# Two of the four transfers that exchange a tile's exponentials move from SyncE's queue to ScalarE's

## The chip, the cores and the metric

The kernel runs on one core of a Trainium2 chip. The metric is the device time of one execution in microseconds, lower is better. Engines are named as in the profile: PE is TensorE, DVE is VectorE, ACT is ScalarE, POOL is GpSimd, SP is SyncE. An engine's name with a q behind it (ACTq, SPq) is its sequencer, which waits, branches and issues DMAs.

## What is computed

x is 8 x 1024 x 1024, ctx 8 x 64 x 1024, everything in f32:

```
x = x + xattn(layernorm(x), ctx, mask)
x = x + ffn(layernorm(x), weight, lora_A, lora_B, router_w)

xattn(h, mem, mask):   scores  = einsum('bsd,bmd->bsm', h, mem) / sqrt(1024)
                       scores  = where(mask[:, None, :], scores, -1e30)
                       readout = einsum('bsm,bmd->bsd', softmax(scores), mem)
                       (zero for a batch entry without a valid key)
ffn(x, weight, ...):   base    = einsum('btd,od->bto', x, weight)
                       probs   = softmax(einsum('btd,ed->bte', x, router_w))
                       the two largest of 8 experts, renormed, into w_dense
                       Ax      = einsum('nd,erd->ner', x_flat, lora_A)     # rank 16
                       out     = base + 2.0 * einsum('ner,ne,eor->no', Ax, w_dense, lora_B)
```

## The kernel before

The 8192 rows of x are 64 tiles of 128 rows, 8 tiles (j = 0 to 7) in each of 8 batch entries. PE multiplies in fp32r: each f32 operand is split in a high part and a low rest, and a product is three matmuls (high x high, high x low, low x high; three, L1097). All weights stay in SBUF. A tile passes through stages that overlap with those of its neighbours; each engine has a step function that is called for every tile in turn (unrolled for the first and last batch entry, in a loop over the others), and within an engine the instructions run strictly in the order written there. Nothing but semaphores ties the engines together.

In step (tile) the engines do work of five tiles. With nxt, nxt2, +3 for the tiles 1, 2 and 3 later:

- PE (step, L1224): the three groups of base columns of the tile, 24 products (L1100 to L1102; group 0 holds the router logits and the LoRA columns too); after an odd j the scores of two later tiles (pair_scores, L1127 and L1129); the readout of nxt2 (L1174 and L1175, weights are eT); lora_second of the tile (weights are hT_hi and hT_lo).
- DVE (step, L986): softmax_split and e_transposes of nxt2, an xT_low, router_top (L929), router_gate (L941 to L960), h_transposes, x2_transposes of nxt (L914), add_readout and norm2_stats of nxt2, hT_low (L968), norm2_moments, x2T_low of nxt (L921), softmax_scores of +3, and the base additions (L984).
- ACT (step, L660): the two exponentials of nxt2 (L581, L583), norm1_mean (L552) and norm1_squares (L559) of +3, gate_exp of the tile (L617), eT_copy of nxt2 (L588), x2T_high of nxt (L613), hT_high of the tile (L623), in an odd j two xT_high, and norm2 of nxt2, which writes xn (L607).
- POOL: the powers and products of both norms, a few elements each.
- SP (step, L424): all transfers. exchange (L375) copies xn to xq in four DMAs; then e_exchange (L411), store (L370), h_exchange (L405), the load of a later tile's x, in an even j s_exchange, in an odd one two loads of xT.

Once per batch entry the context changes: in j = 3 DVE sums the new ctxT and SP has loaded it just before; in j = 4 PE makes the mean (L1107), DVE subtracts it (ctx_centre, L780) between h_transposes and x2_transposes, and ACT makes the high part (ctxT_high, L533) between gate_exp and eT_copy; in j = 5 DVE makes the new mask.

The exchange of the exponentials. A transpose on DVE turns blocks of 32 x 32 only. e_transposes (L869) writes the tile's 128 x 128 values of e_split, turned block by block, into eq, and counts eq_done up. e_exchange then puts the four bands of 32 partitions side by side with four DMAs of 16 KB each:

```
def e_exchange(tile):
    sp.wait_ge(eq_done, count(tile, 1, 1 - 5))
    for i in range(Q):
        sp.dma_start(e_raw[:, i * QP:(i + 1) * QP], eq[i * QP:(i + 1) * QP, :]).then_inc(e_loaded, 16)
```

eT_copy on ACT waits until e_loaded has counted all four (16 * Q per tile) and rounds e_raw into eT, the weights of the readout. The first five tiles are turned on PE instead and have no such exchange. eq and e_raw are parts of the tensor w_raw, so in the profile the transfers read w_raw<-w_raw (L415), and eT_copy reads eT<-w_raw. s_exchange is w_raw<-w_raw too (L421).

norm1_mean and norm1_squares each pass over a tile's 128 x 1024 values; what they write beside their sums goes into x2T, which x2_transposes overwrites later: that one waits until the squares are counted in ln1_step.

Of the kernel before, what the change touches and what calls it, by code (L numbers as in the profile page):

```python
# [23 lines left out]
def xattn_lora_moe_kernel(  # L24
# [17 lines left out]

    P = 128
    NT, _, D = x_in.shape
    NB, _, _, M = ctxT_in.shape
    ER, O = bT_in.shape
    WC = wT_in.shape[2]
# [12 lines left out]
    Q = 4  # L60
    QP = P // Q
# [24 lines left out]
    def count(tile, per, more=0):  # L86

        b, j = tile
        return b * (TPB * per) + (j * per + more)

    def after(tile, n):
        return (tile[0], tile[1] + n)

    def exists(tile):
        return not isinstance(tile[0], int) or tile[0] * TPB + tile[1] < NT

    def turned_on_pe(tile, n):
        return isinstance(tile[0], int) and tile[0] * TPB + tile[1] < n

    def slot(tile):  # L100
        return tile[1] % XS
# [7 lines left out]
    with stack:  # L109
# [6 lines left out]
        def sem(name):  # L116
            return stack.enter_context(nc.semaphore(name))
# [73 lines left out]
        eq = w_raw[0][:, C - 1, P:2 * P]  # L191
        e_raw = w_raw[0][:, C - 1, 2 * P:3 * P]
# [13 lines left out]
        def x(tile):  # L206

            i = slot(tile) - XF
            if i < 0:
                return x_first[:, slot(tile), :]  # L210
            return x_rest[i][:, :, :].rearrange("p c n -> p (c n)")[:, x_from[i]:x_from[i] + D]
# [108 lines left out]
        eq_done = sem("eq_done")  # L320
        e_loaded = sem("e_loaded")
# [28 lines left out]
        def _(sp):  # L350
# [60 lines left out]
            def e_exchange(tile):  # L411

                sp.wait_ge(eq_done, count(tile, 1, 1 - 5))
                for i in range(Q):
                    sp.dma_start(e_raw[:, i * QP:(i + 1) * QP], eq[i * QP:(i + 1) * QP, :]).then_inc(e_loaded, 16)  # L415

            def s_exchange(tile):
# [6 lines left out]
            def step(tile, first=False):  # L424
# [4 lines left out]
                if exists(after(tile, 3)) and not first and not turned_on_pe(after(tile, 3), 5):  # L429
                    e_exchange(after(tile, 3))  # L430
# [99 lines left out]
        def _(act):  # L530
            def ctxT_high(b):
                act.wait_ge(ctx_centred, b + 1)
                act.copy(ctxT[:, :, 0:M], ctxT_raw[:, :, :]).then_inc(ctxT_hi_done, 1)  # L533

            def ctx_high(b):
                act.wait_ge(ctx_loaded, b * 16 + 16)
                if isinstance(b, int) and b == 0:
                    act.wait_ge(ctx_rest_loaded, 16)
                act.wait_ge(readout_done, count((b, 0), 2))
                act.copy(ctx_hi[:, :], ctx_raw[:, 0:D]).then_inc(ctx_hi_done, 1)  # L540

            def norm1_mean(tile):
                b, j = tile
                xs = x(tile)
                junk = x2T[:, :, :].rearrange("p c n -> p (c n)")
                act.wait_ge(x_loaded[slot(tile)], b * (16 * TPB // XS) + 16 * (j // XS + 1))
                if isinstance(b, int) and tile == (0, 0):
                    act.wait_ge(x_rest_loaded[0], 16)
                act.wait_ge(rstd1_done, count(tile, 1))
                if not isinstance(b, int) or b > 0 or j > 1:  # L550
                    act.wait_ge(x2T_split, count(tile, 2, -4))
                act.activation(junk, xs, ACT.Identity, scale=-1.0 / D, accum_out=neg_mean1[:, :]).then_inc(ln1_step, 1)  # L552

            def norm1_squares(tile):

                xs = x(tile)
                junk = x2T[:, :, :].rearrange("p c n -> p (c n)")
                act.wait_ge(ln1_step, count(tile, 2, 1))
                act.activation(junk, xs, ACT.Square, bias=neg_mean1[:, :], accum_out=sum_sq1[:, :]).then_inc(ln1_step, 1)  # L559

            def xT_high(tile, i):
                b, j = tile
                k = j // 2 % 2
                act.wait_ge(xT_loaded[k][i], b * (16 * TPB // 4) + 16 * (j // 4 + 1))
                if isinstance(b, int) and tile == (0, 0):
                    act.wait_ge(xT_rest_loaded[i], 16)
                act.wait_ge(sT_done, pairs(tile, 1))
                act.copy(xT_hi[:, i], xT_raw[:, k, i]).then_inc(xT_hi_done, 1)  # L568
# [6 lines left out]
            def softmax_exp(tile):  # L575
                act.wait_ge(softmax_step, count(tile, 5, 3))
                if turned_on_pe(tile, 6):
                    act.wait_ge(eT_done, count(tile, 1))
                else:
                    act.wait_ge(eq_done, count(tile, 1, -5))  # L580
                act.activation(e_all[:, :], s_all[:, :], ACT.Exp, bias=neg_max[:, :],  # L581
                               accum_out=e_sum[:, :]).then_inc(exp_done, 1)
                act.activation(e_split[:, 0:M], s_all[:, :], ACT.Exp, bias=neg_max[:, :]).then_inc(exp_done, 1)  # L583

            def eT_copy(tile):
                act.wait_ge(e_loaded, count(tile, 16 * Q, 16 * Q * (1 - 5)))
                act.wait_ge(readout_done, count(tile, 2))
                act.copy(eT[:, :], e_raw).then_inc(eT_copied, 1)  # L588

            def first_softmax_exp(tile):  # L590
                act.wait_ge(softmax_step, count(tile, 5, 3))
                act.wait_ge(e_split_done, count(tile, 1))
                act.wait_ge(x1_done, count(tile, 2))
                act.wait_ge(eT_done, count(tile, 1))
                act.activation(e_all[:, :], s_all[:, :], ACT.Exp, bias=neg_max[:, :],
                               accum_out=e_sum[:, :]).then_inc(exp_done, 1)
                act.activation(first_e(0), by_blocks(s_all[:, :]), ACT.Exp, bias=neg_max[:, :]).then_inc(exp_done, 1)

            def first_eT_copy(tile):
                act.wait_ge(eT_done, count(tile, 1, 1))  # L600
                act.wait_ge(readout_done, count(tile, 2))
                act.copy(eT[:, :], et_ps).then_inc(eT_copied, 1)

            def norm2(tile):
                act.wait_ge(shift2_done, count(tile, 1, 1))
                act.wait_ge(x2T_done, count(tile, TS))
                act.activation(xn[:, :], x(tile), ACT.Identity, bias=shift2[:, :],  # L607
                               scale=rstd2[:, :]).then_inc(xn_done, 1)

            def x2T_high(tile):  # L610
                act.wait_ge(x2T_done, count(tile, TS, TS))
                for i in range(2):
                    act.copy(chunks(xT2_hi[:, tile[1] % 2], i), chunks(x2T, i)).then_inc(x2T_hi_done, 1)  # L613

            def gate_exp(tile):
                act.wait_ge(router_step, count(tile, 7, 1))
                act.activation(gate_num[:, :], top8[:, 0:1], ACT.Exp, bias=top8[:, 1:2],  # L617
                               scale=-1.0).then_inc(gate_exp_done, 1)

            def hT_high(tile):  # L620
                act.wait_ge(h_loaded, count(tile, 16 * Q, 16 * Q * (1 - 2)))
                act.wait_ge(base_done, count(tile, G))
                act.copy(hT_hi[:, :], h[:, :]).then_inc(hT_hi_done, 1)  # L623
# [36 lines left out]
            def step(tile):  # L660
                b, j = tile
                nxt, nxt2 = after(tile, 1), after(tile, 2)
                if turned_on_pe(nxt2, 5):
                    first_softmax_exp(nxt2)
                elif exists(nxt2):
                    softmax_exp(nxt2)
                if exists(after(tile, 3)):
                    norm1_mean(after(tile, 3))
                    norm1_squares(after(tile, 3))
                gate_exp(tile)  # L670
                if j == TPB - 4 and exists((b, TPB)):
                    ctxT_high(b + 1)
                if turned_on_pe(nxt2, 5):
                    first_eT_copy(nxt2)
                elif exists(nxt2):
                    eT_copy(nxt2)
                if exists(nxt):
                    x2T_high(nxt)
                hT_high(tile)
                if j == TPB - 3 and exists((b, TPB)):  # L680
                    ctx_high(b + 1)
                if j % 2 == 1 and exists(after(tile, 5)):
                    for i in range(2):
                        xT_high(after(tile, 5), i)
                if exists(nxt2):
                    norm2(nxt2)
# [701 lines left out]
```

## Time and profile before

| | |
|---|---|
| median of 3 runs | 984.8 us (983.56 to 985.69) |
| profiled execution | 983.3 us, span 981.2 us |
| PE busy | 973.7 us (99%) |
| PE weight loads busy | 961.7 us (98%) |
| DVE busy | 850.0 us (87%) |
| ACT busy | 474.5 us (48%) |
| POOL busy | 144.2 us (15%) |
| DMA | 160 GB/s in the mean |

The span runs from the first instruction to the last one's end. A matmul's duration in the rows below (about 0.33 us) is longer than its distance to the next one (about 0.16 us), since they are pipelined; distances are read from starts. Rows of a timeline give the start in us from the span's start, the duration, engine, line, operation, out<-in, shape and count, and in brackets how long the engine was idle before it and what ended that.

### The profile page before, as it was taken

What the parts mean: (1) busy time and instruction counts of PE and PEld (TensorE: products, weight loads), DVE (VectorE), ACT (ScalarE), POOL (GpSimd) and SP (SyncE); (2) the same over time, 40 slices, a digit from 0 to 9 for tenths busy, and PEclk for the clock granted to TensorE, in tenths of its full rate; (3) what the DMA queues carried; (4) which work ended last, traced back from release to release, by engine and by line L of the source; (5) the groups of instructions that cost most, each with busy time, mean ns of one, the idle gap of its engine ahead of it and who ended that gap; (6) DMA issues with size and microseconds to landing.
All of it is one profiled execution on the core that took longest, in us unless ns stands there. A gap on an engine that the chain in (4) does not pass through costs nothing.

```text
span 981.2 us, 18824 instructions
## 1 busy us (share of the span) xinstructions
PE 973.7 (99%) x6081; PEld 961.7 (98%) x6081; DVE 850.0 (87%) x2201; ACT 474.5 (48%) x930; POOL 144.2 (15%) x278
## 2 busy tenths in 40 slices
PE   8999999999999999999999999999999999999998
PEld 7999999999999999999999999999999999999998
DVE  6988988889888998889988899888998889888774
ACT  6755544545444455445455445454454454453420
POOL 3311111111111111111111111111111111111110
PEclk9999999999999999999999999999999999999999
DMA  9646565655566555565555755556655566554522
GB/s 323 216 131 166 157 172 159 179 132 153 165 175 181 164 124 160 165 193 157 154 137 156 203 138 169 140 140 196 162 161 163 124 191 168 160 159 127 122 67 76
DMA packets 156095, 156.61 MB, mean 160 GB/s; under 512 B 93968, under 2 KB 128912, under 8 KB 156048
## 3 DMA queue, kind: packets, MB, share of 16 engines
q1 hardware_dynamic: 155184, 154.63, 56.8%
q10 hardware_dynamic: 864, 1.45, 0.4%
q8 instruction: 18, 0.29, 0.1%
q14 instruction: 29, 0.24, 0.1%
HBM read 78.74 MB, written 33.55 MB: 114 GB/s over the span
## 4 chain that ended last, share of the span: by engine, by line
PE 89%; DVE 5%; DMA 2%; issue 1%; SPq 1%; ACT 1%; POOL 0%; ACTq 0%; DVEq 0%; POOLq 0%
PE base_ps L1100 26%; PE base_ps L1101 25%; PE base_ps L1102 25%; PE ro_ps L1174 3%; PE ro_ps L1175 3%; PE s_ps L1129 2%; PE s_ps L1127 2%; PE base_ps L1206 1%; DMA xq<-xn 1%; DVE stats L898 1%; DMA xT_raw<-in_xT 1%; DVE x2T L914 1%; DVE w_raw L892 1%; SPq L379 1%; ACT xn L607 0%
## 5 line engine op out<-in xcount | busy, mean ns | idle before, releaser
L1100 PE MATMUL base_ps<-w_hi,xT_hi 128*128 128x392 f32 x1512 | 495.5, 328 | 0.0
L1101 PE MATMUL base_ps<-w_lo,xT_hi 128*128 128x392 f32 x1512 | 494.4, 327 | 0.0
L1102 PE MATMUL base_ps<-w_hi,xT_lo 128*128 128x392 f32 x1512 | 494.4, 327 | 0.0
L1100 PEld LDWEIGHTS base_ps<-w_hi,xT_hi 128*128 128x128 f32 x1512 | 285.8, 189 | 1.7
L1101 PEld LDWEIGHTS base_ps<-w_lo,xT_hi 128*128 128x128 f32 x1512 | 285.8, 189 | 1.6
L1102 PEld LDWEIGHTS base_ps<-w_hi,xT_lo 128*128 128x128 f32 x1512 | 285.8, 189 | 0.0
L914 DVE STREAM_TRANSPOSE x2T<-xq 128x512 f32<-128x512 f32 x122 | 166.1, 1465 | 19.7 <-DMA xq<-xn 19.4
L492 POOL TENSOR_TENSOR rstd<-var_eps,neg_half 128x1 f32<-128x1 f32 x64 | 61.8, 966 | 504.1 <-DVE var_eps L905 504.1
L613 ACT CAST xT_hi<-x2T 128x512 fp32r<-128x512 f32 x122 | 69.5, 617 | 106.2 <-DVE x2T L914 106.2
L588 ACT CAST eT<-w_raw 128x128 fp32r<-128x128 f32 x59 | 17.6, 299 | 151.7 <-DMA w_raw<-w_raw 151.7
L921 DVE TENSOR_TENSOR xT_lo<-x2T,xT_hi 128x512 fp32r<-128x512 f32 x122 | 78.3, 682 | 0.0
L607 ACT ACTIVATE xn<-w_raw,shift,rstd 128x1024 f32<-128x1024 f32 x32 | 39.7, 1241 | 70.9 <-POOL shift L495 70.9
L814 DVE TENSOR_TENSOR xT_parts<-xT_raw,xT_parts 128x1024 fp32r<-128x1024 f32 x62 | 73.4, 1186 | 0.0
L607 ACT ACTIVATE xn<-x_first,shift,rstd 128x1024 f32<-128x1024 f32 x29 | 36.0, 1241 | 69.4 <-POOL shift L495 69.4
L568 ACT CAST xT_parts<-xT_raw 128x1024 fp32r<-128x1024 f32 x64 | 63.8, 1042 | 0.0
L1100 PE MATMUL base_ps<-b_hi,hT_hi 128*128 128x384 f32 (+1 forms) x192 | 59.7, 311 | 0.9 <-DVE hT_lo L968 0.9
L1102 PE MATMUL base_ps<-b_hi,hT_lo 128*128 128x384 f32 (+1 forms) x192 | 59.3, 309 | 0.0
L1101 PE MATMUL base_ps<-b_lo,hT_hi 128*128 128x384 f32 (+1 forms) x192 | 59.3, 309 | 0.0
L486 POOL TENSOR_TENSOR var_eps<-sum_sq,eps_sum 128x1 f32<-128x1 f32 x64 | 17.4, 272 | 277.8 <-ACT x2T L559 276.8
L1129 PE MATMUL s_ps<-xT_parts,ctxT 128*128 128x256 f32 x232 | 53.3, 275 | 0.0
L1127 PE MATMUL s_ps<-xT_parts,ctxT 128*128 128x256 f32 x232 | 53.2, 275 | 0.0
L929 DVE MAX8 top<-base_ps 128x8 f32<-128x8 f32 x64 | 11.1, 173 | 45.0 <-PE base_ps L1102 44.3
(132 smaller groups left out, 1391.5 us busy)
## 6 DMA issues: line engine op xcount, KB each, us to landing
xT_raw<-in_xT SPq DMA_DIRECT2D x62, 512.0 KB, 5.3
xq<-xn SPq DMA_DIRECT2D x244, 128.0 KB, 3.5
w_raw<-in_x SPq DMA_DIRECT2D x32, 512.0 KB, 3.5
out<-x_first SPq DMA_DIRECT2D x32, 512.0 KB, 2.7
out<-w_raw SPq DMA_DIRECT2D x31, 512.0 KB, 2.8
x_first<-in_x SPq DMA_DIRECT2D x30, 512.0 KB, 3.6
h<-w_raw SPq DMA_DIRECT2D x248, 16.0 KB, 2.0
w_raw<-w_raw SPq DMA_DIRECT2D x236, 16.0 KB, 2.6
```

What stands on the lines that cost most here:

```text
L492: pool.tensor_tensor(rstd2[:, :], var_eps2[:, :], neg_half[:, :], ALU.pow).then_inc(rstd2_done, 1)
L568: act.copy(xT_hi[:, i], xT_raw[:, k, i]).then_inc(xT_hi_done, 1)
L607: act.activation(xn[:, :], x(tile), ACT.Identity, bias=shift2[:, :], scale=rstd2[:, :]).then_inc(xn_done, 1)
L613: act.copy(chunks(xT2_hi[:, tile[1] % 2], i), chunks(x2T, i)).then_inc(x2T_hi_done, 1)
L814: dve.tensor_tensor(xT_lo[:, i], xT_raw[:, tile[1] // 2 % 2, i], xT_hi[:, i].bitcast(f32), ALU.subtract).then_inc(xT_split, 1)
L914: dve.transpose(out_[:, i * QS:(i + 1) * QS], xq[:, i * QS:(i + 1) * QS, :].rearrange("p g (c n) -> p g c n", n=QP)).then_inc(x2T_done, 1)
L921: dve.tensor_tensor(chunks(xT2_lo[:, k], i), chunks(x2T, i), chunks(xT2_hi[:, k], i).bitcast(f32), ALU.subtract).then_inc(x2T_split, 1)
L1100: pe.matmul(out_, a_hi, w_h, start=start, stop=False, skip_group_check=again)
L1101: pe.matmul(out_, a_hi, w_l, start=False, stop=False, skip_group_check=again)
L1102: return pe.matmul(out_, a_lo, w_h, start=False, stop=stop, skip_group_check=again)
L1127: pe.matmul(s_ps[:, 0:T2], ctxT[:, c, :], xT_hi[:, :, c, :].rearrange("p t n -> p n t"), start=(c == 0), stop=False)
L1129: mm = pe.matmul(s_ps[:, 0:T2], ctxT[:, c, :], xT_lo[:, :, c, :].rearrange("p t n -> p n t"), start=False, stop=(c == C - 1))
```

## The change

SP issues the first two of the four transfers of e_exchange; the last two are issued by ACT, between norm1_mean and norm1_squares of its step, after a wait of its own for eq_done. The count that eT_copy waits for is the same.

```diff
@@ block.sync, e_exchange @@
                 sp.wait_ge(eq_done, count(tile, 1, 1 - 5))
-                for i in range(Q):
+                for i in range(Q // 2):
                     sp.dma_start(e_raw[:, i * QP:(i + 1) * QP], eq[i * QP:(i + 1) * QP, :]).then_inc(e_loaded, 16)
@@ block.scalar @@
+            def e_exchange(tile):
+                act.wait_ge(eq_done, count(tile, 1, 1 - 5))
+                for i in range(Q // 2, Q):
+                    act.dma_start(e_raw[:, i * QP:(i + 1) * QP], eq[i * QP:(i + 1) * QP, :]).then_inc(e_loaded, 16)
+
@@ block.scalar, step @@
                 if exists(after(tile, 3)):
                     norm1_mean(after(tile, 3))
+                if exists(nxt2) and not turned_on_pe(nxt2, 5):
+                    e_exchange(nxt2)
+                if exists(after(tile, 3)):
                     norm1_squares(after(tile, 3))
                 gate_exp(tile)
```

ACT's instructions in the step j = 4 of the first batch entry, before. The names are those of the lists above; top is the sorted logits, ctxT the context's high part:

```order
L581 ACTIVATE e_all,e_sum<-s_all,neg_max 128x64 [waits eq_done,softmax_step]
L583 ACTIVATE e_split<-s_all,neg_max 128x64
L552 ACTIVATE x2T,neg_mean<-w_raw 128x1024 [waits x2T_split,rstd1_done,x_loaded7]
L559 ACTIVATE x2T,sum_sq<-w_raw,neg_mean 128x1024 [waits ln1_step]
L617 ACTIVATE gate_num<-top 128x1 [waits router_step]
L533 CAST ctxT<-ctxT_raw 128x8x64 [waits ctx_centred]
L588 CAST eT<-w_raw 128x128 [waits readout_done,e_loaded]
```

The same place with the change:

```order
L581 ACTIVATE e_all,e_sum<-s_all,neg_max 128x64 [waits eq_done,softmax_step]
L583 ACTIVATE e_split<-s_all,neg_max 128x64
L552 ACTIVATE x2T,neg_mean<-w_raw 128x1024 [waits x2T_split,rstd1_done,x_loaded7]
L588 DMA w_raw<-w_raw 128x1x32 [waits eq_done]
L588 DMA w_raw<-w_raw 128x1x32
L559 ACTIVATE x2T,sum_sq<-w_raw,neg_mean 128x1024 [waits ln1_step]
L622 ACTIVATE gate_num<-top 128x1 [waits router_step]
L533 CAST ctxT<-ctxT_raw 128x8x64 [waits ctx_centred]
L593 CAST eT<-w_raw 128x128 [waits readout_done,e_loaded]
```

Two issues with a wait for eq_done stand between the passes; the rest keeps its order (lines below the insertion have numbers that are 5 higher).

SP's queue in one step with an odd j, before (xq<-xn is exchange, L415 e_exchange, out the store, h the h_exchange):

```order
L379 DMA xq<-xn 32x4x256 [waits xn_done]
L379 DMA xq<-xn 32x4x256 x3
L415 DMA w_raw<-w_raw 128x1x32 [waits eq_done]
L415 DMA w_raw<-w_raw 128x1x32 x3
L373 DMA out<-x_first 128x1024 [waits out_done]
L409 DMA h<-w_raw 128x1x32 [waits hq_done]
```

And with the change:

```order
L379 DMA xq<-xn 32x4x256 [waits xn_done]
L379 DMA xq<-xn 32x4x256 x3
L415 DMA w_raw<-w_raw 128x1x32 [waits eq_done]
L415 DMA w_raw<-w_raw 128x1x32
L373 DMA out<-x_first 128x1024 [waits out_done]
L409 DMA h<-w_raw 128x1x32 [waits hq_done]
```

The store and h_exchange follow after two issues of e_exchange instead of four.

## Rows read from the trace of the kernel before

**Rows 1.** Windows: stretch, length; busy us (count) of PE, PEld, DVE, ACT, POOL; PEclk, DMA, GB/s.

```profile
360.00:480.00 120.00, 120.00 (x754) 119.14 (x754) 107.05 (x277) 59.00 (x116) 16.85 (x32) 1.00 0.59 161
```

**Rows 2.** Waits of the whole span: engine, line, awaited: us in total, times, longest.

```profile
ACT eT L588 <- DMA w_raw<-w_raw: 151.7, 52, 4.4
...
DVE hT_lo L968 <- ACT hT_hi L623: 5.7, 3, 4.1
...
PEld ro_ps L1174 <- ACT eT L588: 1.6, 5, 0.4
```

**Rows 3.** Timeline of PE: the first matmul of the readout in two long steps.

```profile
410.82 0.38 PE L1174 MATMUL ro_ps<-ctx_hi,eT 128*128 128x512 f32 x1
...
440.52 0.38 PE L1174 MATMUL ro_ps<-ctx_hi,eT 128*128 128x512 f32 x1
```

**Rows 4.** Timeline of ACT through an ordinary long and short step.

```profile
400.96 1.24 ACT L607 ACTIVATE xn<-x_first,shift,rstd 128x1024 f32<-128x1024 f32 x1 [3.02 <-POOL shift L495]
...
405.66 0.30 ACT L617 ACTIVATE gate_num<-top 128x1 f32<-128x1 f32 x1 [0.57 <-DVE top L929]
...
416.34 1.24 ACT L607 ACTIVATE xn<-x_first,shift,rstd 128x1024 f32<-128x1024 f32 x1 [2.08 <-POOL shift L495]
...
419.00 0.19 ACT L552 ACTIVATION_READ_ACCUMULATOR x2T<-w_raw 128x1 f32 x1
...
421.40 0.29 ACT L617 ACTIVATE gate_num<-top 128x1 f32<-128x1 f32 x1 [0.93 <-DVE top L929]
...
430.65 1.24 ACT L607 ACTIVATE xn<-w_raw,shift,rstd 128x1024 f32<-128x1024 f32 x1 [3.03 <-POOL shift L495]
```

**Rows 5.** Timeline of DVE through the same two steps.

```profile
407.67 2.61 DVE L914 STREAM_TRANSPOSE x2T<-xq 128x512 f32<-128x512 f32 x2
411.02 0.45 DVE L873 STREAM_TRANSPOSE w_raw<-s_ps 128x256 f32<-128x256 f32 x1 [0.74 <-PE s_ps L1129]
...
418.59 0.31 DVE L869 STREAM_TRANSPOSE w_raw<-e_split 128x128 f32<-128x128 f32 x1
...
423.32 2.76 DVE L914 STREAM_TRANSPOSE x2T<-xq 128x512 f32<-128x512 f32 x2
...
428.48 0.27 DVE L968 TENSOR_TENSOR hT_lo<-h,hT_hi 128x128 fp32r<-128x128 f32 x1
```

**Rows 6.** Timeline of PE's weight loads: the first of lora_second in that short step.

```profile
429.38 0.19 PEld L1100 LDWEIGHTS base_ps<-b_hi,hT_hi 128*128 128x128 f32 x1
```

**Rows 7.** One line's instructions (ns min/median/max), and the page's issues (median us to landing).

```profile
L415 SPq DMA_DIRECT2D w_raw<-w_raw x236: 542/605/1117, 77.5 to 943.3; - x118
...
w_raw<-w_raw SPq DMA_DIRECT2D x236, 16.0 KB, 2.6
```

**Rows 8.** Timeline of ACT and of PE's weight loads in a step j = 4.

```profile
451.09 0.29 ACT L617 ACTIVATE gate_num<-top 128x1 f32<-128x1 f32 x1 [0.48 <-DVE top L929]
...
454.21 0.29 ACT L588 CAST eT<-w_raw 128x128 fp32r<-128x128 f32 x1
...
454.56 0.19 PEld L1174 LDWEIGHTS ro_ps<-ctx_hi,eT 128*128 128x128 f32 x1
```

**Rows 9.** Timeline of ACT at the start: the first of its six issues, and its first work.

```profile
0.74 0.41 ACTq L688 DMA_DIRECT2D ctxT_raw<-in_ctxT  x1
...
3.69 1.28 ACT L695 ACT_TABLE_LOAD   x1 [3.69 <-issue]
```

**Rows 10.** Timeline of ACT and PE's weight loads in another step j = 4.

```profile
213.13 0.30 ACT L617 ACTIVATE gate_num<-top 128x1 f32<-128x1 f32 x1
...
216.60 0.19 PEld L1174 LDWEIGHTS ro_ps<-ctx_hi,eT 128*128 128x128 f32 x1 [0.42 <-ACT eT L588]
```

**Rows 11.** Timeline of ACT and DVE in the steps j = 5 and j = 6.

```profile
465.33 0.28 ACT L617 ACTIVATE gate_num<-top 128x1 f32<-128x1 f32 x1
...
468.15 2.64 DVE L914 STREAM_TRANSPOSE x2T<-xq 128x512 f32<-128x512 f32 x2 [0.46 <-DMA xq<-xn]
...
481.01 0.30 ACT L617 ACTIVATE gate_num<-top 128x1 f32<-128x1 f32 x1 [1.04 <-DVE top L929]
```

## The prediction

> **What bounds the kernel now.** The page in the table above says that PE is busy 973.7 of 981.2 us, DVE 850.0, ACT 474.5. The windows say whether that leaves slack anywhere in the middle: in a stretch of 120 us PE is busy 120.00, at a granted clock of 1.00 [rows 1]. The waits come next: in the middle of the kernel PE waits only for five weight loads of the readout that eT holds up, 1.6 us in all [rows 2]. So PE sets the time. What helps another engine can give back little more than those 1.6 us; what makes PE wait is paid in full.
>
> The question is how closely the others follow PE. An even j takes a short step, an odd one a long step (with pair_scores). From one long step's readout to the next PE takes 440.52 - 410.82 = 29.70 us [rows 3]. Beside it runs a ring of ACT, DVE and POOL that closes once per step: xn (L607), exponentials, the two passes of norm 1, gate_exp (L617), router_gate, x2_transposes (L914), readout and stats, POOL, and the next xn. I walk it by the starts in the timeline and take out the idle time in which an engine waited for something that PE decides:
> - long step: from xn at 400.96 to gate_exp at 405.66, less 0.57 idle, 4.13; to x2T at 407.67, 2.01; to the next xn at 416.34, 8.67, less 0.74 in which DVE waited for PE's scores, 7.93. Sum 14.07 [rows 4, 5].
> - short step: from 416.34 to 421.40 less 0.93, 4.13; to x2T at 423.32, 1.92; to xn at 430.65, 7.33. Sum 13.38 [rows 4, 5].
>
> The ring needs 27.45 us in each 29.70 of PE: 2.25 us are free in two steps. PE meets the ring's work at three places, the weight loads of the readout (after eT), of lora_second (after hT_lo) and of the next base. hT_lo ends at 428.48 + 0.27 = 428.75 and the load behind it starts at 429.38 [rows 5, 6]: 0.63 us of margin.
>
> **The change, part by part.** SP loses two of four small issues per tile, 605 ns each by the median [rows 7], so 1.21 us. xq is issued ahead of e_exchange and stays where it was. Behind it the store and h_exchange move up; neither is worth anything, for hT_lo waited for ACT's side of that path 5.7 us in three places only [rows 2]. What is won is eT: ACT waits for its data 151.7 us in 52 places [rows 2], and the last transfer is now issued some 1.2 us earlier. That shortens ACT's idle time. PE has of it only what lies in late readouts outside the step j = 4; one of 0.42 lies inside [rows 10], and I take 0.6 of the 1.6 for the rest. Gain: 0.6 us.
>
> ACT gains one wait and two issues in every step, between mean and squares. On ACT the squares, gate_exp and all later work are queued behind them; router_gate and x2_transposes on DVE wait for gate_exp. The wait costs nothing in an ordinary step: the transposed exponentials end at 418.59 + 0.31 = 418.90, before the mean's accumulator read starts at 419.00 [rows 4, 5]. For the issues no row shows a small SBUF-to-SBUF transfer on ACT's queue. The nearest are the same transfer on SP, 542 to 1117 ns, median 605 [rows 7], and ACT's six larger loads at the start, the first 0.41, all six from 0.74 to 3.69, when ACT's first work starts [rows 9]: an issue holds ACT. I take the same transfer's 2 x 0.605 = 1.21, less 0.06 beside the accumulator read: **1.15 us per step**. The bounds are 0.82 (2 x 0.41) and 2.23 (2 x 1.117), and below these nothing, should ACT compute on while it issues.
>
> That time is not spare. The ring becomes 27.45 + 2 x 1.15 = 29.75 against PE's 29.70. An ordinary pair of steps breaks even: late, inside the 0.63 margin, with nothing left to catch up. So whatever stretches the ring once per batch reaches PE, and seven batches have these steps:
> - j = 4. ctx_centre and ctxT_high (L533) stand between the gate and eT. gate_exp had 0.48 of idle, so it comes 1.15 - 0.48 = 0.67 later, and all behind it moves along: L533, then eT, which ended at 454.21 + 0.29 = 454.50, with PE's weight load at 454.56 [rows 8]. There is no margin; PE waits 0.67. In three of the seven (the one near 213 stands in [rows 10]; also near 570 and 690) gate_exp had no idle and eT was late already: there all of 1.15 is paid. 4 x 0.67 + 3 x 1.15 = 6.1 us.
> - j = 5 and 6. In j = 5 gate_exp had no idle, so it is 1.15 later, of which x2T's 0.46 of waiting for xq absorbs a part: 0.69. In j = 6 gate_exp had 1.04: 0.11 more [rows 11]. That makes 0.80 against 0.63 at lora_second: 0.17 x 7 = 1.2 us.
>
> Sum: 6.1 + 1.2 - 0.6 = **+6.7 us**. The profiled execution took 983.3 us, so 990.0 for it; the median of the three runs shown is 984.8, which gives **991.5**.
>
> The Trainium skill, "DMA: Bandwidth & Descriptors", section "Issuing engines are not separate DMA queues", says that starting DMAs on several engines saves only the sequencer's time to start them, which is usually small beside the DMA. By it alone, nothing would be won or paid. This trace does not agree on "small": 0.605 us of issue beside 2.6 to landing [rows 7], and it is paid on an engine that has the ring behind it.
>
> **The rivals.**
> - Cheap issue: 0.41 each, 0.82 per step, as ACT's loads at the start. Against it: the median of SP's issues of just this kind is half as long again. The ring is 29.09 and recovers between batches; the steps j = 4 remain: 4 x (0.82 - 0.48) + 3 x 0.82 = 3.8, less 0.6: +3.2, 988.0. Chance 0.22.
> - Dear issue: ACT issues while SP issues xq, and the two slow each other to 1.117 each. The ring is 27.45 + 4.46 = 31.91, 2.21 over PE in each of 29 pairs (236 / 4 = 59 tiles): +64, 1049. Against it: at the start both queues issue side by side at 0.41 to 0.54, and 1.117 is one of 236 [rows 7, 9]. Chance 0.08.
> - Not slower: ACT's engine works on while the issues run, or they slip under the mean's pass. Then only the earlier eT is left, 0.6 to 1.6 off: 983.2 to 984.2. It decides if less than 0.48 per step is added, the idle time in j = 4. For it: the exponentials are ready before the mean is done. Against it: ACT takes its queue in order, and [rows 9]. Chance 0.17, 0.04 of it for a gain over 2 us, which PE's waits hardly hold. The rule of the Trainium skill above would come out here too.
> - The ring as forecast: 0.53. Within it, 1.27 per step instead of 1.15 makes 29.99, 0.29 over PE in 29 pairs: 8 us more, 1000.
>
> **How the numbers follow.** The likeliest case gives 991.5. The range 984.0 to 1003.0 leaves out the dear issue (0.08) and about half of the case without cost (0.09). A measurement of this kernel can tell some 0.2%, 2 us, from no change. Slower by more: ring, cheap and dear issue, less 0.03 that fall short of it, 0.80. Within: 0.16. Faster by more: 0.04.
>
> **What would show it.** In the profile after: two issues on ACT's queue per step between L552 and L559, about 0.6 each, and L559's start 1.2 us later behind L552; ACT's idle time before gate_exp nearly gone; DVE idle behind gate_exp; ACT's wait for eT's data down by half or more; and PE's weight loads waiting for eT in all seven steps j = 4, 0.7 to 1.2 each, and at times for hT_lo. I am wrong if the issues on ACT take under 0.4, if L559 does not move, or if the time grows while PE's waits stay at 1.6 us.

## The result, and the profile after

The changed kernel takes 991.15 us (median of 6 runs, 989.92 to 993.95) against 984.69 of the kernel before on the same chip; the ratio is 1.0070, 95% interval 1.0059 to 1.0081. That is 6.5 us more. 991.5 was forecast.

The page of the kernel after, its busy times:

```profile
span 989.6 us, 18848 instructions
...
PE 973.1 (98%) x6081; PEld 959.2 (97%) x6081; DVE 850.2 (86%) x2201; ACT 464.8 (47%) x930; POOL 141.6 (14%) x278
```

No engine has more work than before (DVE's 850.2 against 850.0 is the largest difference upwards). The span is 8.4 us longer than the 981.2 before, and PE is busy as long as it was; so the time came as idle time of PE. The window that answers to [rows 1]:

```profile
360.00:480.00 120.00, 118.86 (x745) 117.70 (x744) 105.40 (x276) 56.37 (x114) 16.13 (x32) 1.00 0.60 160
```

PE lost 1.14 us in these 120 us, at the same granted clock. The stretch is as long as one batch entry and holds one step j = 4. The waits (engine, line, awaited: us in total, times, longest) say for whom it waits; line numbers are 5 (ACT) or 8 (DVE, PE) higher than before:

```profile
ACT eT L593 <- DMA w_raw<-w_raw: 129.9, 52, 3.8
...
ACT x2T L559 <- issue: 66.4, 58, 1.6
...
DVE gate_den L949 <- ACT gate_num L622: 23.6, 37, 1.1
DVE x2T L922 <- DMA xq<-xn: 19.5, 40, 1.4
...
ACT gate_num L622 <- DVE top L937: 12.4, 4, 6.3
PEld ro_ps L1182 <- ACT eT L593: 10.5, 10, 1.7
...
PEld base_ps L1108 <- DVE hT_lo L976: 1.8, 3, 1.3
```

PE's weight loads wait 10.5 us for eT where they waited 1.6 [rows 2]: 8.9 us more, while the span grew by 8.4. Two rows lead up to it. ACT stands idle ahead of the squares (L559) for 66.4 us in 58 steps, behind the issues, and gate_den on DVE, which never waited for gate_num before, does so for 23.6 us. One row refutes a step of the forecast: ACT still waits 129.9 us for the data of eT, against 151.7, where half or less was forecast.

The timeline of ACT in an ordinary short step, the counterpart of [rows 4]:

```profile
419.65 1.24 ACT L612 ACTIVATE xn<-x_first,shift,rstd 128x1024 f32<-128x1024 f32 x1 [1.90 <-POOL shift L495]
...
421.37 1.04 ACT L552 ACTIVATE x2T<-w_raw 128x1024 f32<-128x1024 f32 x1
422.24 0.57 ACTq L588 DMA_DIRECT2D w_raw<-w_raw  x1
...
422.85 0.62 ACTq L588 DMA_DIRECT2D w_raw<-w_raw  x1
423.58 1.15 ACT L559 ACTIVATE x2T<-w_raw,neg_mean 128x1024 f32<-128x1024 f32 x1 [1.08 <-issue]
...
424.74 0.28 ACT L622 ACTIVATE gate_num<-top 128x1 f32<-128x1 f32 x1
...
427.35 0.30 ACT L593 CAST eT<-w_raw 128x128 fp32r<-128x128 f32 x1 [2.33 <-DMA w_raw<-w_raw]
```

The first issue starts at 422.24, beside the end of the mean (421.37 + 1.04 = 422.41). The squares start 2.21 us after the mean. Before they did so after 1.16:

```profile
418.06 1.04 ACT L552 ACTIVATE x2T<-w_raw 128x1024 f32<-128x1024 f32 x1
...
419.22 1.15 ACT L559 ACTIVATE x2T<-w_raw,neg_mean 128x1024 f32<-128x1024 f32 x1
...
424.06 0.30 ACT L588 CAST eT<-w_raw 128x128 fp32r<-128x128 f32 x1 [2.37 <-DMA w_raw<-w_raw]
```

So ACT is held 1.05 us. That is about the idle time of 0.93 that gate_exp had in this step: no bracket stands behind L622 any more, and it starts 3.37 us after the mean (424.74 - 421.37), where it started 3.34 after it before (421.40 - 418.06). The last row says what became of the gain. From xn to eT_copy it took 424.06 - 416.34 = 7.72 us before and takes 427.35 - 419.65 = 7.70 now. The data of eT is there not a bit earlier. The instructions of one line, ACT's issues:

```profile
L588 ACTq DMA_DIRECT2D w_raw<-w_raw x118: 550/616/894, 75.7 to 948.8; - x118
...
DMA to landing us min/median/max: 3.1/3.5/4.1
```

An issue costs ACT 616 ns, where it cost SP 605 [rows 7]. But eT_copy waits for the last of the four transfers, and that is none of ACT's: in all 59 exchanges SP's second lands last now, as SP's fourth did before. This last transfer in the step shown, after and then before:

```profile
L415 SPq DMA_DIRECT2D w_raw<-w_raw x1: 617/617/617, 424.3 to 424.3; - x1
...
DMA to landing us min/median/max: 3.0/3.0/3.0
```

```profile
L415 SPq DMA_DIRECT2D w_raw<-w_raw x1: 602/602/602, 422.1 to 422.1; - x1
...
DMA to landing us min/median/max: 1.8/1.8/1.8
```

It was issued 5.8 us after xn's start and is issued 4.6 us after it now (422.1 - 416.34 and 424.3 - 419.65), 1.2 earlier as forecast; but it takes 3.0 us to land where it took 1.8. Both sums are 7.6. The last xq transfer lands later too, 5.95 us after xq's first issue in the median, against 5.58. Which part of the DMA side holds the eight transfers to the same end isn't shown.

The step j = 4 that answers to [rows 8], from the timeline of ACT, DVE and PE's weight loads:

```profile
452.17 1.04 ACT L552 ACTIVATE x2T<-w_raw 128x1024 f32<-128x1024 f32 x1
...
453.12 0.30 DVE L877 STREAM_TRANSPOSE w_raw<-e_split 128x128 f32<-128x128 f32 x1
...
453.46 1.27 ACTq L588 DMA_DIRECT2D w_raw<-w_raw  x2
...
454.84 1.15 ACT L559 ACTIVATE x2T<-w_raw,neg_mean 128x1024 f32<-128x1024 f32 x1 [1.54 <-issue]
...
455.99 0.28 ACT L622 ACTIVATE gate_num<-top 128x1 f32<-128x1 f32 x1
...
456.30 0.15 DVE L949 TENSOR_SCALAR gate_den<-gate_num 128x1 f32<-128x1 f32 x1 [1.09 <-ACT gate_num L622]
...
458.44 0.62 ACT L533 CAST ctxT<-ctxT_raw 128x512 fp32r<-128x512 f32 x1 [2.18 <-DVE ctxT_raw L788]
458.97 0.29 ACT L593 CAST eT<-w_raw 128x128 fp32r<-128x128 f32 x1
459.31 0.19 PEld L1182 LDWEIGHTS ro_ps<-ctx_hi,eT 128*128 128x128 f32 x1 [1.44 <-ACT eT L593]
```

Here the transposed exponentials end at 453.42, 0.2 us behind the mean (453.21), and the issue waits for them: the squares start 2.67 us after the mean, 1.50 later than before (449.37 - 448.20 = 1.17). gate_exp is late by more than its idle time, DVE waits 1.09 at gate_den, and the chain L788, L533, eT hands the lateness on to PE, which waits 1.44.

### The profile page after: what moved, and what is told of

The parts are those of the page before. It is cut to its first block, busy times and chain, and to the rows that moved or that the text cites. A ratio compares the mean times of both kernels' runs of the same rounds, so it can differ in the third digit from the quotient of the medians.

```text
span 989.6 us, 18848 instructions
## 1 busy us (share of the span) xinstructions
PE 973.1 (98%) x6081; PEld 959.2 (97%) x6081; DVE 850.2 (86%) x2201; ACT 464.8 (47%) x930; POOL 141.6 (14%) x278
## 4 chain that ended last, share of the span: by engine, by line
PE 30%; DVE 23%; issue 16%; DMA 13%; POOL 5%; ACT 5%; SPq 5%; ACTq 2%; POOLq 0%; DVEq 0%
DMA xq<-xn 12%; PE base_ps L1108 8%; PE base_ps L1110 8%; PE base_ps L1109 8%; DVE stats L906 5%; SPq L379 5%; DVE x2T L922 5%; POOL rstd L492 4%; ACT xn L612 3%; DVE w_raw L900 3%; DVE x_first L900 2%; ACTq L588 1%; PE base_ps L1214 1%; POOL shift L495 1%; PE ro_ps L1182 1%
## 5 line engine op out<-in xcount | busy, mean ns | idle before, releaser
L922 DVE STREAM_TRANSPOSE x2T<-xq 128x512 f32<-128x512 f32 x122 | 164.6, 1453 | 20.0 <-DMA xq<-xn 19.5
L593 ACT CAST eT<-w_raw 128x128 fp32r<-128x128 f32 x59 | 17.6, 298 | 129.9 <-DMA w_raw<-w_raw 129.9
L486 POOL TENSOR_TENSOR var_eps<-sum_sq,eps_sum 128x1 f32<-128x1 f32 x64 | 13.5, 211 | 341.1 <-ACT x2T L559 340.1
L1182 PE MATMUL ro_ps<-ctx_hi,eT 128*128 128x512 f32 x128 | 49.9, 390 | 7.7 <-ACT eT L593 7.6
L559 ACT ACTIVATE x2T<-w_raw,neg_mean 128x1024 f32<-128x1024 f32 x32 | 36.8, 1150 | 35.9 <-issue 35.8
L1137 PE MATMUL s_ps<-xT_parts,ctxT 128*128 128x256 f32 x232 | 53.3, 275 | 0.0
```

The costliest lines, as they stand in the source:

```text
L922: dve.transpose(out_[:, i * QS:(i + 1) * QS], xq[:, i * QS:(i + 1) * QS, :].rearrange("p g (c n) -> p g c n", n=QP)).then_inc(x2T_done, 1)
L1137: mm = pe.matmul(s_ps[:, 0:T2], ctxT[:, c, :], xT_lo[:, :, c, :].rearrange("p t n -> p n t"), start=False, stop=(c == C - 1))
L1182: pe.matmul(half(ro_ps, i), eT[:, :], in_turn(half(ctx_hi, i)), start=True, stop=False)
```

## The experiments

Two theories had to be told apart. The ring: what costs is that ACT is held ahead of gate_exp, and with it DVE. The rival: what costs is the DMA side, two queues at a time, with xq and the exponentials landing later. Within the ring it was open which steps pay, and at which place. Each run is set against runs of the kernel before that were made beside it: medians of 984.38 us for e1 to e4, 984.04 for e5 to e8, 983.21 for e9 to e12.

### e1: ACT held by work, no transfer moved

```diff
                 if exists(after(tile, 3)):
                     norm1_mean(after(tile, 3))
+                    if not turned_on_pe(nxt2, 5):
+                        for t, n, s in [(hold_a, H, hold_sum_a), (hold_b, P, hold_sum_b)]:
+                            act.activation(t[:, :], x(after(tile, 3))[:, 0:n], ACT.Identity, scale=1.0, accum_out=s[:, :])
                     norm1_squares(after(tile, 3))
```

> All four transfers stay on SP. Between the first norm's passes ACT runs two extra activations over 512 and 128 columns with sums that nothing reads (about 1.1 us together), so ACT is held as long as by the two issues, but no transfer moves. Theory of the ring (what costs is the time that ACT is held ahead of gate_exp): the loss of the change comes back, +5 to +8 us over the kernel before, with PE's weight loads waiting for eT in the steps j = 4. Rival (what costs is the DMA side: transfers on a second queue slow xq and land later): no loss, within 1 us of before.

Measured: 987.33 us, ratio 1.0028 (1.0015 to 1.0040), +2.95 us by the medians. The activations (512 and 128 columns) came out shorter than meant. From the timeline:

```profile
420.06 1.04 ACT L556 ACTIVATE x2T<-w_raw 128x1024 f32<-128x1024 f32 x1
...
422.00 1.14 ACT L563 ACTIVATE x2T<-w_raw,neg_mean 128x1024 f32<-128x1024 f32 x1
```

The squares start 1.94 us after the mean, so the hold is 0.78 and not 1.05. A hold without any transfer costs time, which the rival can't explain; whether it explains all of it took e5 and e9. (The cheap-issue rival of the prediction, 0.82 per step, was priced at +3.2.)

### e2: ACT only waits

```diff
                     norm1_mean(after(tile, 3))
+                if exists(nxt2) and not turned_on_pe(nxt2, 5):
+                    act.wait_ge(eq_done, count(nxt2, 1, 1 - 5))
+                if exists(after(tile, 3)):
                     norm1_squares(after(tile, 3))
```

> All four transfers stay on SP; ACT gets only the wait for eq_done between the passes, no issue. Ring: nothing is held but 0.05 to 0.1 us in the steps j = 4, so 0 to +1 us. Rival (the wait itself delays ACT, since the transposed exponentials come as the mean ends): most of the 6.5 us.

Measured: 984.12 us, ratio 0.9994 (0.9985 to 1.0003). The wait by itself costs nothing that can be measured.

### e3 and e4: eT_copy ahead of ctxT_high in the steps j = 4

Both with this edit, e3 on the changed kernel, e4 on the kernel before:

```diff
-                if j == TPB - 4 and exists((b, TPB)):
-                    ctxT_high(b + 1)
                 if turned_on_pe(nxt2, 5):
                     first_eT_copy(nxt2)
                 elif exists(nxt2):
                     eT_copy(nxt2)
+                if j == TPB - 4 and exists((b, TPB)):
+                    ctxT_high(b + 1)
```

> The changed kernel, with eT_copy ahead of ctxT_high on ACT in the steps j = 4. Ring theory, in which PE pays because eT stands behind ctxT_high, and that behind the gate and ctx_centre on DVE: the waits for eT in these steps fall from about 1.4 us to under 0.3, and the time to 984.5 to 987. Rival (eT is late because its data lands late, 3.5 us after the issue on ACT's queue): eT and the time stay as they are, 990 to 991.

> The kernel before, with eT_copy ahead of ctxT_high in the steps j = 4. Ring theory: the waits for eT there go (three of the five were there, about 1.1 us): 0.5 to 1.5 us faster than before. Rival (ctxT_high then comes late and the next batch's scores wait): 0 to +2 us.

Measured: e3 991.42 us, ratio 1.0063 (1.0049 to 1.0077), nothing gained. e4 983.81, ratio 1.0001 (0.9990 to 1.0012). My expectation for e3 failed, and so did the rival's: eT is no longer late. The waits of e3:

```profile
PEld base_ps L1108 <- DVE hT_lo L976: 10.1, 14, 1.2
...
PEld ro_ps L1182 <- ACT eT L593: 4.5, 13, 0.6
```

The wait for eT went down from 10.5 to 4.5, and the wait for hT_lo up from 1.8 to 10.1. (This profiled execution is the slowest of the five, 994.06 us.) The order of two copies on ACT only chose where PE meets the late ring. In a step j = 4 PE waits 0.42 for the readout's weights and, 5.8 us on, 1.06 for DVE's product hT_lo:

```profile
458.44 0.19 PEld L1182 LDWEIGHTS ro_ps<-ctx_hi,eT 128*128 128x128 f32 x1 [0.42 <-ACT eT L593]
...
464.23 0.19 PEld L1108 LDWEIGHTS base_ps<-b_hi,hT_hi 128*128 128x128 f32 x1 [1.06 <-DVE hT_lo L976]
```

What is late is DVE, and the place at which PE stands idle isn't the cause.

### e5: the full hold

As e1, with activations over 384, 64, 64 and 64 columns (squares 2.26 us after the mean, a hold of 1.10).

```diff
+                        for t, n, s in holds:
+                            act.activation(t[:, :], x(after(tile, 3))[:, 0:n], ACT.Identity, scale=1.0, accum_out=s[:, :])
```

> As e1, with four small activations, so that the squares start 1.05 us later, as they do in the changed kernel (in e1 they start 0.78 later, and that cost 2.8 us). All transfers on SP. Theory that ACT's hold is the whole cost: +6 to +7 us. Rival, that part of the cost comes from the transfers on ACT's queue (the last xq transfer lands 4.00 us after its issue in the changed kernel instead of 3.63, and x2_transposes wait): +3.5 to +5, and xq lands at 3.63.

Measured: 988.51 us, ratio 1.0053 (1.0033 to 1.0072), +4.5 us by the medians. That lies in the rival's range of 3.5 to 5, and my 6 to 7 lies in the upper part of the interval (3.2 to 7.1), so it settled nothing and rather spoke for the rival. What the expectation had overlooked: the hold is that of an ordinary step, 1.10, while the changed kernel holds ACT 1.50 in j = 4.

### e6: the issues behind gate_exp

```diff
-                if exists(nxt2) and not turned_on_pe(nxt2, 5):
-                    e_exchange(nxt2)
                 if exists(after(tile, 3)):
                     norm1_squares(after(tile, 3))
                 gate_exp(tile)
+                if exists(nxt2) and not turned_on_pe(nxt2, 5):
+                    e_exchange(nxt2)
```

> The changed kernel, with ACT's wait and its two issues moved behind gate_exp, ahead of eT_copy. Ring theory: nothing ahead of gate_exp is held, so DVE is on time and the waits of gate_den for gate_num go; the data of eT lands later than before, which can make PE's readout wait in short steps: -0.5 to +4 us. Rival (two queues at once are the cost, wherever the issues stand): +5 to +7.

Measured: 1002.69 us, ratio 1.0197 (1.0180 to 1.0214), +18.7 us, well beyond what either theory said. The waits:

```profile
ACT eT L593 <- DMA w_raw<-w_raw: 186.1, 59, 5.4
...
PEld ro_ps L1182 <- ACT eT L593: 21.2, 33, 1.6
```

DVE's wait for gate_num is gone from the list, as the ring has it; but now the data of eT is late in all steps and PE waits in 33 of them. That the data would land later was expected; the price of it was far too low. I had not worked out that the issue moves behind router_top: ACT's first issue starts 5.07 us after xn's start in the median, in the changed kernel 2.59.

### e7 and e8: only the steps j = 4, and all but them

```diff
+    SHARED = 6
@@ SP's e_exchange @@
-                for i in range(Q // 2):
+                for i in range(Q // 2 if tile[1] % TPB == SHARED else Q):
@@ ACT's step @@
-                if exists(nxt2) and not turned_on_pe(nxt2, 5):
+                if nxt2[1] % TPB == SHARED and exists(nxt2) and not turned_on_pe(nxt2, 5):
                     e_exchange(nxt2)
```

e7 is this (nxt2 has j = 6 where ACT is in step 4); e8 has != in both places.

> ACT issues two of the four only in the steps j = 4 (8 of 59 tiles); in all others SP issues four. If the price of the change is what ACT's hold does in these steps alone: +5 to +6.5 us. If it is the lateness that the other steps build up and that j = 4 only brings to light: +1 to +3.

> The counterpart of e7: ACT issues two of the four in every step but j = 4. First theory of e7: 0 to +1.5 us. Second: +3.5 to +5.5.

Measured: e7 991.21 us, ratio 1.0077 (1.0061 to 1.0094). e8 985.05, ratio 1.0011 (0.9999 to 1.0022). Eight steps carry the whole price (e7 is +7.2 us by the medians, a little over its +5 to +6.5). 51 steps with the same two issues are free or nearly so: +1.0 us by the medians, with an interval from 0 to 2.2. The waits of e7, then of e8:

```profile
ACT x2T L560 <- issue: 11.6, 8, 1.5
PEld ro_ps L1183 <- ACT eT L594: 11.3, 12, 1.4
...
DVE gate_den L950 <- ACT gate_num L623: 7.0, 7, 1.1
```

```profile
ACT x2T L560 <- issue: 55.5, 50, 1.4
...
DVE gate_den L950 <- ACT gate_num L623: 18.9, 30, 1.0
PEld base_ps L1109 <- DVE hT_lo L977: 3.3, 6, 1.2
PEld ro_ps L1183 <- ACT eT L594: 2.9, 8, 0.6
```

In e8 gate_den waits 18.9 us, more than twice the 7.0 of e7, and PE hardly notices. In e7 about as much as the 7.0 is paid. A wait on DVE costs only where its step has no slack to take it up.

### e9: ACT held by work in the steps j = 4 alone

```diff
                     norm1_mean(after(tile, 3))
+                    if nxt2[1] % TPB == 6:
+                        for t, n, s in holds:
+                            act.activation(t[:, :], x(after(tile, 3))[:, 0:n], ACT.Identity, scale=1.0, accum_out=s[:, :])
                     norm1_squares(after(tile, 3))
```

> All transfers on SP. Only in the steps j = 4, ACT runs six small activations between the passes, about 1.45 us, as long as the changed kernel holds ACT there (its squares start 1.50 us later in these steps, 1.05 in the others). If ACT's hold in eight steps is the whole price: +6 to +7.5 us, as e7. If the transfers on ACT's queue have a part in it: +3 to +4.5.

Measured: 990.76 us, ratio 1.0080 (1.0067 to 1.0093). The hold in the timeline:

```profile
450.00 1.04 ACT L554 ACTIVATE x2T<-w_raw 128x1024 f32<-128x1024 f32 x1
...
452.59 1.13 ACT L561 ACTIVATE x2T<-w_raw,neg_mean 128x1024 f32<-128x1024 f32 x1
```

2.59 us from mean to squares, a hold of 1.42 in eight steps, all transfers where they were, gives the whole price of the change: +7.55 us by the medians, where e7, with the same hold and the transfers, gave +7.2. The rival has no part in it that can be measured; the intervals leave room for some 2 us. e5 fits too: it held ACT in j = 4 for 1.10 only.

### e10: all four on ACT

```diff
@@ SP's e_exchange: nothing is left @@
-                sp.wait_ge(eq_done, count(tile, 1, 1 - 5))
-                for i in range(Q // 2):
-                    sp.dma_start(e_raw[:, i * QP:(i + 1) * QP], eq[i * QP:(i + 1) * QP, :]).then_inc(e_loaded, 16)
@@ ACT's e_exchange @@
-                for i in range(Q // 2, Q):
+                for i in range(Q):
```

> All four transfers issued by ACT between the passes, none by SP. The hold is 1.05 + 2 x 0.63 = 2.3 us in every step. Ring theory: 27.45 + 4.6 = 32.1 us for two steps against PE's 29.70, 2.4 more in each of 29 pairs: +60 to +75 us, with PE waiting in every pair. Rival (only j = 4 has a price, in proportion to the hold): +13 to +18.

Measured: 1051.04 us, ratio 1.0696 (1.0679 to 1.0712), +67.8 us, within the 60 to 75 of the ring. The waits:

```profile
ACT x2T L559 <- issue: 156.6, 58, 3.8
...
DVE gate_den L949 <- ACT gate_num L622: 109.6, 59, 3.4
...
PEld ro_ps L1182 <- ACT eT L593: 51.1, 37, 3.3
```

Every one of the 59 gates is late now. The sum over the ring (27.45 + 4.6 against 29.70 us) holds where the ring is really the longer of the two: the first pair of issues costs 6.5 us, the second 61. Two things beside the hold differ here. The data of eT lands later, as in e6: xn to eT_copy takes 8.59 us in the median (e6 8.67, the kernel before 7.75). But DVE, which would carry that back into the ring, waits for the readout only 1.1 us in 3 places:

```profile
DVE w_raw L900 <- PE ro_ps L1183: 1.1, 3, 0.5
```

And PE's granted clock is 0.992, where it is 1.000 before; what share that has was not measured.

### e11 and e12: gate_exp ahead of the squares

On the changed kernel (e11) and on the kernel before (e12, without the issues):

```diff
                 if exists(nxt2) and not turned_on_pe(nxt2, 5):
                     e_exchange(nxt2)
+                gate_exp(tile)
                 if exists(after(tile, 3)):
                     norm1_squares(after(tile, 3))
-                gate_exp(tile)
```

> The changed kernel with gate_exp ahead of norm1_squares: mean, two issues, gate_exp, squares. The squares (1.15 + 0.1 us) no longer stand ahead of the gate; x2_transposes needs them only 2.1 us after the squares' end. If the price is gate_exp's lateness: the waits of gate_den for gate_num go and the time is 983 to 985.5. If ACT's total load or the transfers cost: 988 to 991.

> The kernel before with the same exchange of gate_exp and squares, no transfer moved. ACT now waits for router_top before the squares, about 1 us. Its own lateness at j = 4 (no idle in three of seven) goes: -1.5 to 0 us. It becomes slower only if the late squares hold up x2_transposes.

Measured: e11 983.64 us, ratio 1.0005 (0.9995 to 1.0014). e12 983.97, ratio 1.0009 (0.9999 to 1.0019). The waits of e11:

```profile
ACT gate_num L622 <- DVE top L937: 112.2, 63, 6.3
ACT eT L593 <- DMA w_raw<-w_raw: 96.2, 52, 3.3
DVE x2T L922 <- DMA xq<-xn: 37.6, 47, 1.9
...
PEld ro_ps L1182 <- ACT eT L593: 1.6, 5, 0.4
```

With the same two issues on ACT the loss is gone. gate_exp waits for DVE again (112.2 us), DVE for gate_exp nowhere, and PE's waits for eT are back at the 1.6 us of before. So the two issues are free once the gate doesn't stand behind them and the squares together: it still stands behind the issues, but ahead of the squares' 1.15 us. That the order alone isn't worth the 7 us regained is what e12 shows (+0.8 by the medians, not clear of nothing). The issues are also worth nothing: neither version beats the kernel before. x2_transposes now waits 37.6 us for xq, against 19.5 in the changed kernel.

## Why the prediction was right, and where its terms were off

- **The mechanism.** "That time is not spare": shown. The hold alone gives the price (e9), without it the wait gives none (e2), and putting gate_exp ahead of the squares, whose 1.15 us it then no longer waits for, gives the price back (e11).
- **The hold.** 1.15 us per step was forecast from SP's 605 ns, less 0.06 beside the accumulator read, whose working is missing. It is 1.05 (616 ns each on ACT, begun while the mean still runs). The cheap issue (0.82) and the dear one (2.23) are refuted; so is the case that was not slower. The Trainium skill, "DMA: Bandwidth & Descriptors", section "Issuing engines are not separate DMA queues", says that several issuing engines save only the time of issuing. This trace agrees that nothing more is saved: the last of the four transfers landed 7.6 us after xn's start in both kernels. The page calls that time "usually small relative to the DMA itself"; here it was 0.616 us beside 3.5 to landing, paid by an engine that others wait for.
- **"An ordinary pair of steps breaks even"**: e8 bears it out, 51 such steps for 1.0 us by the medians (0 to 2.2), and e10 from the other side.
- **The steps j = 4.** Forecast 4 x 0.67 + 3 x 1.15 = 6.1 us; PE's wait for eT grew by 8.9 us in the profiled execution, and in all seven steps PE waits, as forecast, by 1.05 to 1.68 us each where 0.7 to 1.2 was said. "The wait costs nothing" is wrong for this step: the exponentials come 0.2 us after the mean there, so the hold is 1.50. With that the forecast's own sum gives 4 x (1.50 - 0.48) + 3 x 1.50 = 8.6. The idle time in it is rough: one of the four steps (near 809) had 0.05 and not 0.48, and in the step shown after, PE waits 1.44, as if none of the 0.48 had been left. Lateness from issues in the other steps isn't needed for that: e7 has no issues in them, and PE waits 1.43 there in the same step. In the three steps without idle time the wait grew by 0.92 to 1.12 and not by 1.50. What sets the single steps stays open.
- **The steps j = 5 and 6.** Forecast 1.2 us. Nothing shows: the waits for hT_lo went from 1.5 to 1.8 us. A reason that no run tests by itself is that PE's own stop in j = 4 gives the ring its time back: I had kept the lateness of the ring and forgotten that PE was now late too.
- **The gain.** 0.6 us were forecast for an earlier eT. There is none: 7.72 and 7.70 us from xn to eT_copy. The reading that failed is that an issue 1.2 us earlier is data 1.2 us earlier: the last transfer is issued that much earlier, and takes 3.0 us to land in place of 1.8.
- **The sum is better than its parts, by luck.** The forecast is 1.1 (e7) to 2.8 us (the waits in the profile) too low in j = 4, and 0.6 too low for the gain that didn't come; it is 1.2 too high in j = 5 and 6. The medians differ by 6.5 us, but the two profiled executions by 8.3 (983.3 and 991.62), and the same 6.7 were forecast for both.
- **Where PE meets the ring.** I put the price on eT behind ctxT_high. In the trace it stands there, but e3 shows that this place is exchangeable: the wait moved to hT_lo and the time stayed.

## What to carry to other kernels

A few issues on a compute engine cost nearly their full issue time (here 0.6 us each) to all that stands behind them in its program. Look for the closed ring around the bounding engine, add up its busy pieces per period, and ask of each step by itself how much idle time it has: the price came from 8 of 59 steps. Where a wait of the bounding engine has been found, a reordering that removes it from that place proves nothing until the time has moved too; e11's order, which computes the late engine's input ahead of work that nobody was waiting for, was the one that did. And where data comes in several transfers, follow the one that lands last, not the ones that were moved.

## What the runs showed of the hardware that was not expected

- A DMA issue on ACT starts while the activation ahead of it is running (422.24 beside an end at 422.41), but the next activation does not start before the issues have ended: 0.57 and 0.62 us, then L559 0.11 us later.
- Two issues given to a second queue did not complete the set of transfers sooner. The last of the four was issued 1.2 us earlier, on SP's queue, and landed 3.0 us after its issue in place of 1.8. ACT's two, issued while SP issued xq's, took 3.5 us to land (3.1 to 4.1).
- xq lands a little later: the page's median from issue to landing went from 3.5 to 3.6 us. DVE waits for it 40 times instead of 27, but no longer in total (19.5 and 19.4 us).
- ACT's issue time is that of SP: 550/616/894 ns against 542/605/1117.
